# Half of the key transposes moved from TensorE to VectorE and DMA, and the convolution's taps shared by ScalarE and VectorE

## The chip, the cores and the metric

The kernel runs on one core of a Trainium2 chip. The metric is the time of one execution on the device in microseconds (us); lower is better. One profiled execution gives the rows below; its span runs from the first to the last instruction of the program.

## The reference

The input x has 8 sequences of 2048 tokens with 256 channels, in f32. Each token is normalised (xn), and the output is x + attention(xn) + ffn(xn).

- Attention: q, k, v = xn @ wqkv; q and k pass a relu; 16 heads of 16 channels. It is causal linear attention: for each token, num = q . cumsum(k v^T), den = q . cumsum(k) + 1e-5, y = num / den, and y @ wo.
- FFN: a router of 8 scores (sigmoid of xn @ Wr) picks the best two per token and scales them to a sum of one. Four of the eight experts are MLPs, silu(xn @ Wg) * (xn @ Wu) @ Wd with 128 hidden channels; two more give xn, one gives relu(xn), one gives nothing. To this a causal depthwise convolution of four taps over the tokens is added, with a bias: conv[n] = b + sum over i of w[i] * xn[n - 3 + i].

## The kernel before

The work goes in 32 batches of 512 tokens (T = 4 tiles of 128), four batches to a sequence; I number them 0 to 31. `rounds` (L229) calls one function `batch(s, j, left)` per engine for every batch; all loops are unrolled, and each engine has its own order of instructions, tied to the others by semaphores. `at` (L235) turns a batch and a count into the value of a semaphore. Inside a batch the argument k says for which batch a step works: k = 0 the present one, k = 1 the next, k = 2 or 3 those behind.

TensorE's batch (L433 to L556) has three stages:

1. For each tile t of four (tile and expert have the same number): `gate_up(t)`, twelve products of 512 columns in three passes of high and low halves into two ring banks; then `numerators(t)`, which holds many small products (L466, L482) and two `state_sum` steps (L429). `numerators(t)` waits for silu(t) of ScalarE. Behind tile 0 stand the second half of the masked scores (L415).
2. `heads(s, j, 1)` (L366) for the next batch: value and router products, then two key projections into score banks 0 and 1 and two query projections, and then the key transposes: eight of 128x128 (L397, T = 4 for each of two groups of channels), since `state_sum` needs keys with tokens on partitions (`ktok`).
3. `output(t)` for four tiles: the convolution is turned (L488), attention and the four experts are added up.

ScalarE (L632): silu, the high halves of hid (`high_hid`) and of y (`high_y`), the first tap with the bias (L654), the copies of the heads out of PSUM, relu terms. Its order is written out in L658 to L689. VectorE (L907): state_bd (L902), the gate product (L924), attend (L933), masks (L895), and taps 1 to 3 of the convolution, each two scalar_tensor_tensor of 128x512 (L916) that add to cT; then the statistics of a later batch, the router (L827), key sums, the products for the denominators, and the additions to x_t (L976). GpSimd: weighing hid by the router, low halves, normalising.

From batch 4 on (`by_blocks`, L248) xn isn't transposed on TensorE. VectorE turns it in blocks of 32x32 (`turn_x`, L850) into xb_t, a view of qks_tok, and SP puts the blocks in place with 32 DMAs of 16 KB per batch (`place_turned`, L302, L311). `products` (L866) waits until these have landed, since it writes qks_tok. SP then waits for the router and spreads its weights (`spread_cw`, L287: four small DMAs to DRAM, and one of 1 MB back), stores the finished batch (L321), waits for that, and loads the batch four ahead (L330).

In batches 3 to 30 TensorE's queue has 38 waits on a semaphore that was reached long ago (L538, FILL = 38), at the top of the batch. Two such waits become one instruction of the queue.

Statistics (VectorE) and `normalise` (GpSimd) for the batch two ahead stand at the end of batches 0 and 1; in batch 1 a second pair, for batch 4, stands behind them, after the last addition to x_t.

Of the kernel before, what the change touches and what calls it, by code (L numbers as in the profile page):

```python
# [16 lines left out]
def layer_kernel(nc, x, wqkv, wo, w_router, router_bias, w_gate, w_up, w_down, conv_w, conv_b,  # L17
# [13 lines left out]
    FILL = 38  # L31
# [18 lines left out]
    with ExitStack() as ctx:  # L50
# [85 lines left out]

        rdT = qks
# [26 lines left out]
        KTB = SB[0:2]  # L164

# [36 lines left out]
        s_ktok = sem("s_ktok")  # L202
        s_qp = sem("s_qp")
# [21 lines left out]
        s_conv = sem("s_conv")  # L225
        s_op = sem("s_op")
# [21 lines left out]
        def by_blocks(s, j, k):  # L248

            return s * BPS + j + k >= BY_PE  # L250

# [19 lines left out]
        def _(sp):  # L271
# [15 lines left out]
            def spread_cw(s, j, k):  # L287

                sp.wait_ge(s_cw, at(s, j, 1, k + 1))
                for b in range(P // BLK):  # L290
                    bs = slice(b * BLK, (b + 1) * BLK)
                    sp.dma_start(cw_rows[:, bs], cwt[b * BLK:b * BLK + E * T, :]).then_inc(cw_out, 16)
                sp.wait_ge(cw_out, at(s, j, 16 * P // BLK, (k + 1) * 16 * P // BLK))
# [8 lines left out]
            def place_turned(s, j, k):  # L302

                sp.wait_ge(s_turn, at(s, j, 1, k + 1 - BY_PE))

                sp.wait_ge(s_halo, at(s, j, 1, k - 1))
                for c in range(C):
                    for a in range(QUADS):
                        for q in range(QUADS):
                            row = xT[q * BLK:(q + 1) * BLK, third(s, j, k), c, LEAD:LEAD + BT]  # L310
                            sp.dma_start(row.rearrange("p (t a n) -> p t a n", t=T, a=QUADS)[:, :, a, :],  # L311
                                         xb_t[a * BLK:(a + 1) * BLK, c, q, :, :]).then_inc(xT_in[c], 16)

            def batch(s, j, left):
                b = s * BPS + j
                if left > 1 and by_blocks(s, j, 2):
                    place_turned(s, j, 2)
                if left:
                    spread_cw(s, j, 1)
                    sp.wait_ge(s_out, at(s, j, T, 2 * T))  # L320
# [15 lines left out]
        def _(pe):  # L336
# [29 lines left out]
            def heads(s, j, k):  # L366
# [19 lines left out]
                if not k:  # L386
                    pe.wait_ge(w_split, EARLY)
                for g in range(C):
# [5 lines left out]
                for g in range(C):  # L394
                    pe.wait_ge(s_kT, at(s, j, C, k * C + g + 1))
                    for t in range(T):
# [22 lines left out]
            def state_sum(s, j, k, n):  # L419
# [4 lines left out]
                t, h = n // 2, n % 2  # L424
                toks = slice(h * HALF, (h + 1) * HALF)
# [7 lines left out]
            def batch(s, j, left):  # L433
# [101 lines left out]
                if not last and by_blocks(s, j, 1):  # L535


                    for _ in range(FILL):  # L538
                        pe.wait_ge(tables_in, 16)
# [28 lines left out]
        def _(act):  # L568
# [28 lines left out]
            def heads(s, j, k):  # L597
# [13 lines left out]
                for g in range(C):  # L611
                    act.wait_ge(s_ktr, at(s, j, C, k * C + g + 1))
                    copy(ktok[:, :, g, :], KTB[g][:, :].rearrange("p (t n) -> p t n", t=T)).then_inc(s_ktok, 1)
# [18 lines left out]
            def batch(s, j, left):  # L632
# [24 lines left out]

                silu(0)  # L658
# [10 lines left out]
                high_y(0)  # L669
                silu(1)  # L670
                high_hid(0)
                high_y(1)
                if not last and not ahead:
                    lead(s, j, 1)
                silu(2)
                if not last and not ahead:
                    for c in range(C):
                        high_x(s, j, 1, c)
                high_hid(1)
                high_y(2)  # L680
                silu(3)
                high_hid(2)
                high_y(3)
# [31 lines left out]
        def _(pool):  # L715
# [34 lines left out]
            def batch(s, j, left):  # L750
# [39 lines left out]
                if left > 1 and not by_blocks(s, j, 2):  # L790
# [11 lines left out]
        def _(dve):  # L802
# [54 lines left out]

            def key_sums(s, j, k):
# [48 lines left out]
            def batch(s, j, left):  # L907
                last = left == 0

                def tap(n):  # L910
                    if n == 1:
# [26 lines left out]
                for t in range(T):  # L938
# [23 lines left out]
                if not last:  # L962
                    router(s, j, 1)
                    key_sums(s, j, 1)
# [104 lines left out]
```

## Time and profile before

| | us |
|---|---|
| median of 3 runs (1308.15 to 1309.69) | 1308.89 |
| the profiled execution | 1308.92 |
| its span | 1307.1 |
| PE busy (24160 matmuls) | 1287.2 (98%) |
| PE weight load | 1116.5 (85%) |
| DVE (VectorE) | 1144.3 (88%) |
| ACT (ScalarE) | 707.8 (54%) |
| POOL (GpSimd) | 830.8 (64%) |

Busy shares are of the span. A row of a timeline is: start in us from the span's start, duration in us, engine, line, operation, tiles written and read, shapes, count, and in brackets idle time of the engine before it with what ended it. Instructions of one kind that overlap are merged into one row, so "x4" with 2.48 us is four from the first start to the last end. DMAs have the engine's name with a q: the row is the time that the issue took in the queue, not the transfer.

### The profile page before, as it was taken

How to read it: one execution, taken by the hardware profiler on the slowest of the kernel's cores; microseconds unless marked ns; L12 is line 12 of the kernel's file. 1: busy time of each engine (PE TensorE's matmuls, PEld its weight loads, DVE VectorE, ACT ScalarE, POOL GpSimd, SP SyncE). 2: the span in 40 equal slices, each digit the busy share in tenths (PEclk: the TensorE clock that was granted, in tenths of full speed). 3: DMA queues.
4: the chain of work that ended last, by engine and by line, in shares of the span. 5: the costliest groups of instructions: out<-in, count | busy, mean ns of one | idle time of the engine just before them, and what ended most of it. 6: DMA issues, size and time to landing. Idle time of an engine off the chain costs nothing.

```text
span 1307.1 us, 55818 instructions
## 1 busy us (share of the span) xinstructions
PE 1287.2 (98%) x24160; PEld 1116.5 (85%) x24160; DVE 1144.3 (88%) x2686; ACT 707.8 (54%) x1487; POOL 830.8 (64%) x673
## 2 busy tenths in 40 slices
PE   5999999999999999999999999999999999999998
PEld 4888888888888888888888888888888888888887
DVE  7988898888898888988888988889888889888885
ACT  5645655455654456554555544565545555445552
POOL 2676665765666756657656667566576566675554
PEclk9999999999999999999999999999999999999999
DMA  5012212222222222222222222221222222222211
GB/s 185 14 56 73 78 50 51 80 78 78 65 61 56 79 78 79 51 51 81 78 79 64 67 51 78 78 78 51 51 80 78 79 64 67 51 78 63 61 35 34
DMA packets 175860, 88.54 MB, mean 68 GB/s; under 512 B 135552, under 2 KB 171264, under 8 KB 171520
## 3 DMA queue, kind: packets, MB, share of 16 engines
q1 hardware_dynamic: 174912, 83.97, 22.6%
q8 instruction: 191, 3.13, 1.0%
q10 hardware_dynamic: 704, 1.01, 0.2%
q14 instruction: 53, 0.43, 0.1%
HBM read 53.18 MB, written 17.04 MB: 54 GB/s over the span
## 4 chain that ended last, share of the span: by engine, by line
PE 95%; DVE 3%; POOL 1%; issue 1%; ACT 0%; DMA 0%; DVEq 0%; POOLq 0%
PE ring L343 51%; PE scores L343 17%; PE ring L466 7%; PE ring L482 6%; PE scores L415 5%; PE state_sum L429 4%; PE ring L488 2%; PE scores L397 2%; DVE sm L895 1%; POOL xn L731 0%; DMA x_t<-in_L_attn_x_dram 0%; PE scores L352 0%; POOL rstd L722 0%; DVE stats L819 0%; POOL x_t L748 0%
## 5 line engine op out<-in xcount | busy, mean ns | idle before, releaser
L757 POOL TENSOR_TENSOR hid<-hid,cwb 128x512 f32<-128x512 f32 x128 | 166.4, 1300 | 181.8 <-DVE hid L924 181.0
L916 DVE SCALAR_TENSOR_TENSOR cT<-xT,conv_ws,cT 128x512 f32<-128x512 f32 x192 | 275.1, 1471 | 0.0
L745 POOL TENSOR_TENSOR x_t<-x_t,same 128x1024 f32<-128x1024 f32 x32 | 76.9, 2404 | 254.9 <-ACT same L618 254.9
L639 ACT ACTIVATE sg<-ring 128x512 f32<-128x512 f32 x128 | 76.6, 599 | 268.5 <-PE ring L343 268.5
L343 PE MATMUL ring<-xl,wgu_h 128*128 128x512 f32 x512 | 213.1, 416 | 0.0
L761 POOL TENSOR_TENSOR hl<-hid,hh 128x512 fp32r<-128x512 f32 x128 | 208.8, 1632 | 0.0
L343 PE MATMUL ring<-xh,wgu_l 128*128 128x512 f32 x512 | 201.0, 393 | 0.3 <-issue 0.3
L343 PE MATMUL ring<-xh,wgu_h 128*128 128x512 f32 x512 | 200.5, 392 | 0.0
L569 ACT ACTIVATE yh<-yT 128x256 fp32r<-128x256 f32 x128 | 53.5, 418 | 246.7 <-DVE yT L933 246.7
L902 DVE TENSOR_TENSOR state_bd<-state_sum,tables_s 128x256 f32<-128x256 f32 x248 | 104.0, 419 | 93.8 <-PE state_sum L429 90.6
L895 DVE TENSOR_TENSOR sm<-scores,causal_s 128x512 f32<-128x512 f32 x256 | 157.7, 675 | 6.0 <-PE scores L415 5.0
L343 PE MATMUL ring<-wd_l,hh 128*128 128x256 f32 x496 | 139.3, 281 | 0.0
L343 PE MATMUL ring<-wd_h,hh 128*128 128x256 f32 x496 | 139.1, 280 | 0.0
L343 PE MATMUL ring<-wd_h,hl 128*128 128x256 f32 x496 | 139.0, 280 | 0.0
L766 POOL TENSOR_TENSOR yl<-yT,yh 128x256 fp32r<-128x256 f32 x128 | 135.3, 1057 | 0.0
L466 PE MATMUL ring<-sm,vp 64*32 64x64 f32 x8192 | 122.2, 225 | 0.0
L343 PEld LDWEIGHTS ring<-xl,wgu_h 128*128 128x128 f32 x512 | 96.1, 188 | 26.1 <-issue 5.5
L343 PEld LDWEIGHTS ring<-xh,wgu_l 128*128 128x128 f32 x512 | 96.4, 188 | 23.1 <-issue 0.8
L343 PEld LDWEIGHTS ring<-xh,wgu_h 128*128 128x128 f32 x512 | 96.6, 189 | 16.6
L466 PEld LDWEIGHTS ring<-sm,vp 64*32 64x32 f32 x8192 | 101.6, 105 | 2.8 <-issue 2.8
L343 PE MATMUL scores<-xh,wqk_h 128*128 128x512 f32 x256 | 100.2, 392 | 0.0
L343 PE MATMUL scores<-xl,wqk_h 128*128 128x512 f32 x256 | 100.2, 391 | 0.0
(134 smaller groups left out, 3453.4 us busy)
## 6 DMA issues: line engine op xcount, KB each, us to landing
cwb<-cw_rows SPq DMA_DIRECT2D x32, 1024.0 KB, 4.6
x_t<-in_L_attn_x_dram SPq DMA_DIRECT2D x32, 512.0 KB, 4.2
out_dram<-x_t SPq DMA_DIRECT2D x31, 512.0 KB, 2.9
xT<-qks_tok SPq DMA_DIRECT2D x896, 16.0 KB, 1.8
cw_rows<-cwt SPq DMA_DIRECT2D x128, 2.0 KB, 1.4
sm<-in_L_attn_wqkv_dram ACTq DMA_DIRECT2D x2, 384.0 KB, 5.0
sm<-in_L_ffn_Wg_dram SPq DMA_DIRECT2D x2, 256.0 KB, 3.8
sm<-in_L_ffn_Wu_dram SPq DMA_DIRECT2D x2, 256.0 KB, 4.6
```

Source lines behind the costliest of these rows:

```text
L343: ins = mm(dst, lhs, rhs, start=first and n == 0, stop=final and n == len(passes) - 1, skip_group_check=not (first and final))
L415: ins = mm(SB[f][h * HALF:(h + 1) * HALF, at_:at_ + P], kT[rows, g, n0:n0 + HALF], qp[rows, g, :, n0:n0 + HALF], start=True, stop=True)
L466: mm(NB2[t % 2][h][BLK * m:BLK * m + BLK, gs], window, sm[toks, t // 2, t % 2, 2 * pair + par, :], start=par == 0 and g == 0, stop=False, ...
L482: ins = mm(NB2[t % 2][h][rows, g * HALF:(g + 1) * HALF], state_bd[:, n % 4, cols], qT[:, g, n0:n0 + HALF], start=False, stop=True, skip_gr ...
L639: act.activation(sg[:, :], GB[t % 2], ACT.Silu).then_inc(s_sg, 1)
L745: pool.tensor_tensor(xb, xb, same[:, :, :], ALU.add).then_inc(s_base1, 1)
L757: pool.tensor_tensor(hid[:, e, :], hid[:, e, :], cwb[:, e, :], ALU.mult).then_inc(s_hid, 1)
L761: pool.tensor_tensor(hl[:, e, :], hid[:, e, :], hh[:, e, :].bitcast(F32), ALU.subtract).then_inc(s_hl, 1)
L766: pool.tensor_tensor(yl[:, :, t * P:(t + 1) * P], yT[:, t % 2, :, :], yh[:, :, t * P:(t + 1) * P].bitcast(F32), ALU.subtract).then_inc(s_y ...
L895: dve.tensor_tensor(heads, SB[f][:, :].rearrange("p (t a n) -> p t a n", a=2, n=HALF), causal2_s[:, :].unsqueeze(1).unsqueeze(1).to_broadc ...
L902: dve.tensor_tensor(state_bd[:, n % 4, :].rearrange("p (g m n) -> p g m n", g=C, m=PPG), ST.unsqueeze(2).to_broadcast([P, C, PPG, BLK]), s ...
L916: ins = dve.scalar_tensor_tensor(out=cT[:, c, :], in0=xT[:, third(s, j, 0), c, LEAD - HALO + n:LEAD - HALO + n + BT], scalar=conv_ws[:, c, ...
```

## The change

The diff, with unrelated context cut:

```diff
-    FILL = 38
+    FILL = 54
+        kb = hid[:, 2, :].rearrange("p (a t g i) -> p a t g i", a=QUADS, t=2, g=C)
+        TB = SB[0:2]
+        def keys_at(s, j, k):
+            return (s * BPS + j + k) * (16 * QUADS * QUADS)
...
 SP, spread_cw, between the four small DMAs and the wait for them:
+                if k:
+                    place_keys(s, j, k, range(1))
...
-            def place_turned(s, j, k):
+            def place_turned(s, j, k, c, quarters):
...
+            def place_keys(s, j, k, quarters):
+                sp.wait_ge(s_kturn, at(s, j, 1, k))
+                for a in quarters:
+                    for q in range(QUADS):
+                        sp.dma_start(ktok[a * BLK:(a + 1) * BLK, 2:4, :, q * BLK:(q + 1) * BLK],
+                                     kb[q * BLK:(q + 1) * BLK, a, :, :, :]).then_inc(ktok_in, 16)
 SP, batch:
-                    place_turned(s, j, 2)
+                    place_turned(s, j, 2, 0, range(QUADS))
+                    place_turned(s, j, 2, 1, range(QUADS // 2))
                 if left:
                     spread_cw(s, j, 1)
+                    place_keys(s, j, 1, range(1, QUADS))
...
 TensorE, heads:
+                if k and by_blocks(s, j, k):
+                    pe.wait_ge(s_conv, at(s, j, HALO, HALO))
                 for g in range(C):
                     project(KB[g][:, :], D + g * P).then_inc(s_kp, 1)
...
-                    for t in range(T):
+                    for t in range(T // 2 if k else T):
                         ins = nc.tensor.transpose(KTB[g][:, t * P:(t + 1) * P], kT[:, g, t * P:(t + 1) * P],
                                                   ident_s[:, :])
 TensorE, state_sum:
+                if n == T and s + j:
+                    pe.wait_ge(ktok_in, keys_at(s, j, k))
 TensorE, batch:
-                if not last and by_blocks(s, j, 1):
-                    for _ in range(FILL):
-                        pe.wait_ge(tables_in, 16)
+                def fill(n):
+                    if not last and by_blocks(s, j, 1):
+                        for _ in range(n):
+                            pe.wait_ge(tables_in, 16)
+                fill(FILL // 3)
...
                     if t == T - 1:
                         scores(s, j, 1, 0)
                         state_sum(s, j, 1, 0)
+                    elif t:
+                        fill(FILL // 3)
                     output(t)
...
 ScalarE, heads:
+                    some = T // 2 if k else T
+                    copy(ktok[:, 0:some, g, :], KTB[g][:, 0:some * P].rearrange("p (t n) -> p t n", t=some)
+                         ).then_inc(s_ktok, 1)
+            def place_turned(s, j, n):
+                if n == 0:
+                    act.wait_ge(s_turn, at(s, j, 1, 3 - BY_PE))
+                    act.wait_ge(s_halo, at(s, j, 1, 1))
+                a, q = QUADS // 2 + n // QUADS, n % QUADS
+                row = xT[q * BLK:(q + 1) * BLK, third(s, j, 2), 1, LEAD:LEAD + BT]
+                act.dma_start(row.rearrange("p (t a n) -> p t a n", t=T, a=QUADS)[:, :, a, :],
+                              xb_t[a * BLK:(a + 1) * BLK, 1, q, :, :]).then_inc(xT_in[1], 16)
 ScalarE, batch:
+                def tap_terms(n):
+                    if n == 1:
+                        act.wait_ge(s_sm, at(s, j, U * ROWS, U * ROWS))
+                    else:
+                        act.wait_ge(s_conv, at(s, j, HALO, n - 1))
+                    for c in range(C):
+                        first = LEAD - HALO + n
+                        ins = act.activation(TB[c][:, :], xT[:, third(s, j, 0), c, first:first + BT], ACT.Copy,
+                                             scale=conv_ws[:, c, n:n + 1])
+                    ins.then_inc(s_tapped, 1)
...
 GpSimd, batch, before weigh(1):
+                if by_blocks(s, j, 3) and not by_blocks(s, j, 2):
+                    normalise(s, j, 2)
...
-                if left > 1 and not by_blocks(s, j, 2):
+                if left > 1 and not by_blocks(s, j, 3):
                     normalise(s, j, 2)
 VectorE:
+            def turn_keys(s, j, k):
+                for g in range(C):
+                    dve.wait_ge(s_kT, at(s, j, C, k * C + g + 1))
+                dve.wait_ge(s_hl, at(s, j, T, 3))
+                for t in range(2):
+                    ins = dve.transpose(kb[:, :, t, :, :].rearrange("p a g i -> p g a i"),
+                                        kT[:, :, (2 + t) * P:(3 + t) * P].rearrange("p g (a n) -> p g a n", n=BLK))
+                ins.then_inc(s_kturn, 1)
+                def add_terms(n):
+                    if n == 1:
+                        dve.wait_ge(s_tap0, at(s, j, 1, 1))
+                    else:
+                        dve.wait_ge(s_conv, at(s, j, HALO, n - 1))
+                    dve.wait_ge(s_tapped, (s * BPS + j - BY_PE + 1) * HALO + n)
+                    for c in range(C):
+                        ins = dve.tensor_tensor(cT[:, c, :], TB[c][:, :], cT[:, c, :], ALU.add)
+                    ins.then_inc(s_conv, 1)
                 def tap(n):
+                    if not last and by_blocks(s, j, 1):
+                        add_terms(n)
+                        return
...
 gate_up(2) waits for the keys of the present batch, whose blocks lay in hid[:, 2]:
+                    if t == 2 and s + j:
+                        dve.wait_ge(ktok_in, keys_at(s, j, 0))
...
                         mask(s, j, 0, 1)
+                        if by_blocks(s, j, 3) and not by_blocks(s, j, 2):
+                            statistics(s, j, 2)
...
-                if left > 1 and not by_blocks(s, j, 2):
+                if left > 1 and not by_blocks(s, j, 3):
                     statistics(s, j, 2)
                 elif left > 2:
                     statistics(s, j, 3)
                 if not last:
                     router(s, j, 1)
+                    turn_keys(s, j, 1)
...
-                if by_blocks(s, j, 3) and not by_blocks(s, j, 2):
-                    statistics(s, j, 3)
```

The keys of tiles 2 and 3 of each next batch are turned by VectorE in blocks of 32x32 into the room of hid's third expert, and 16 DMAs from SP put the blocks in place. TensorE turns tiles 0 and 1 only. In batches 3 to 30 taps 1 to 3 are multiplied by ScalarE into score banks 0 and 1 and added by VectorE. Where SP placed 32 blocks of x, it now places 24, and ScalarE issues the other eight between its activations. ScalarE's order in a batch becomes: silu(1), place 0, high_hid(0), place 1, tap_terms(1), place 2, high_y(1), place 3, silu(2), place 4, high_hid(1), place 5, tap_terms(2), place 6, high_y(2), place 7, silu(3), high_hid(2), tap_terms(3), high_y(3). The filling waits stand at three places, 18 each: at the top of the batch, before output(1) and before output(2). Batch 3's statistics stand inside batch 1, behind the masks of its first tile, and its normalisation before weigh(1); batch 4's take the place that batch 3's had.

## Rows read from the trace of the kernel before

**Rows 1.** The page, part 4: the chain that ended last, share by engine.
```profile
PE 95%; DVE 3%; POOL 1%; issue 1%; ACT 0%; DMA 0%; DVEq 0%; POOLq 0%
```
**Rows 2.** The chain of waits in order of time: start us, us, what.
```profile
617.62 5.48 PE scores L343 x24
657.53 5.48 PE scores L343 x24
663.01 0.87 PE scores L397 x8
```
**Rows 3.** Busy time of each engine in one batch's stretch.
```profile
674.60:714.40 39.80, 39.80 (x755) 34.52 (x753) 35.81 (x85) 21.82 (x46) 26.05 (x22) 1.00 0.26 69
```
**Rows 4.** Timeline of VectorE, batch 16: start us, us, what.
```profile
679.56 1.41 DVE L854 STREAM_TRANSPOSE qks_tok<-xn 128x256 f32<-128x256 f32 x4
...
694.61 3.05 DVE L916 SCALAR_TENSOR_TENSOR cT<-xT,conv_ws,cT 128x512 f32<-128x512 f32 x2
...
699.57 0.18 DVE L830 TENSOR_TENSOR scoreb<-score,bias_s 128x32 f32<-128x32 f32 x1
...
702.63 0.12 DVE L848 TENSOR_TENSOR c<-cw 128x4 f32<-128x4 f32 x1
...
714.76 0.42 DVE L976 TENSOR_TENSOR x_t<-ring,x_t 128x256 f32<-128x256 f32 x1
```
**Rows 5.** Groups of instructions: busy us, mean ns of one, idle before.
```profile
L916 DVE SCALAR_TENSOR_TENSOR cT<-xT,conv_ws,cT 128x512 f32<-128x512 f32 x192 | 275.1, 1471 | 0.0
...
L924 DVE TENSOR_TENSOR hid<-ring,sg 128x512 f32<-128x512 f32 x128 | 87.0, 680 | 0.0
...
L654 ACT ACTIVATE cT<-xT,conv_bs,conv_ws 128x512 f32<-128x512 f32 x64 | 48.3, 804 | 0.0
```
**Rows 6.** Timeline of SP's queue in batch 16, and the page's store.
```profile
681.00 23.90 SPq L311 DMA_DIRECT2D xT<-qks_tok  x32
704.94 1.98 SPq L292 DMA_DIRECT2D cw_rows<-cwt  x4
...
715.21 0.40 SPq L321 DMA_DIRECT2D out_dram<-x_t  x1
...
out_dram<-x_t SPq DMA_DIRECT2D x31, 512.0 KB, 2.9
```
**Rows 7.** Timeline of ScalarE, batch 16.
```profile
686.65 0.60 ACT L639 ACTIVATE sg<-ring 128x512 f32<-128x512 f32 x1 [0.70 <-PE ring L343]
...
691.36 0.60 ACT L639 ACTIVATE sg<-ring 128x512 f32<-128x512 f32 x1 [0.70 <-PE ring L343]
691.86 0.62 ACT L569 ACTIVATE hh<-hid 128x512 fp32r<-128x512 f32 x1
```
**Rows 8.** Timeline of PE, batch 16: first and last gate products.
```profile
674.68 0.43 PE L343 MATMUL ring<-xl,wgu_h 128*128 128x512 f32 x1
...
692.29 0.39 PE L343 MATMUL ring<-xh,wgu_l 128*128 128x512 f32 x1
```
**Rows 9.** First DMA issues; ScalarE's semaphore instruction and the activation it passes.
```profile
0.71 0.43 ACTq L691 DMA_DIRECT2D tables_s<-in_tables_dram  x1
...
0.72 0.43 SPq L272 DMA_DIRECT2D x_t<-in_L_attn_x_dram  x1
...
L638 ACTq EVENT_SEMAPHORE  x96: 17/17/17, 37.8 to 1289.7; - x96
...
37.80 0.42 ACT L569 ACTIVATE yh<-yT 128x256 fp32r<-128x256 f32 x1 [2.23 <-DVE yT L933]
```
**Rows 10.** Source view of the filling waits: ns min/median/max, first and last start.
```profile
L539 PEldq EVENT_SEMAPHORE  x504: 51/51/51, 152.6 to 1233.7; - x168
```
**Rows 11.** Timeline of PE in batch 3, gate_up(1).
```profile
161.54 0.50 PE L343 MATMUL ring<-xh,wgu_l 128*128 128x512 f32 x1 [0.34 <-issue]
```
**Rows 12.** Timeline of batch 2: VectorE and PE.
```profile
119.35 1.43 DVE L854 STREAM_TRANSPOSE qks_tok<-xn 128x256 f32<-128x256 f32 x4 [1.60 <-POOL xn L731]
...
123.53 0.33 PE L429 MATMUL state_sum<-vp,ktok 64*32 64x32 f32 x16 [1.19 <-DVE state_bd L902]
```
**Rows 13.** Timeline of VectorE in batch 1.
```profile
80.90 0.42 DVE L902 TENSOR_TENSOR state_bd<-state_sum,tables_s 128x256 f32<-128x256 f32 x1 [0.79 <-PE state_sum L429]
```

More of the change, by code:

```diff
@@ L202, in layer_kernel @@
         s_ktok = sem("s_ktok")
+        s_kturn = sem("s_kturn")
+        ktok_in = sem("ktok_in")
         s_qp = sem("s_qp")
@@ L225, in layer_kernel @@
         s_conv = sem("s_conv")
+        s_tapped = sem("s_tapped")
         s_op = sem("s_op")
@@ L300, in spread_cw @@
                              cw_rows.rearrange("r n -> (r n)").partition_broadcast(P)).then_inc(cw_in, 16)
-            def place_turned(s, j, k):
+            def place_turned(s, j, k, c, quarters):
                 sp.wait_ge(s_turn, at(s, j, 1, k + 1 - BY_PE))
                 sp.wait_ge(s_halo, at(s, j, 1, k - 1))
[L307 to L312, printed above, removed]
+                for a in quarters:
+                    for q in range(QUADS):
+                        row = xT[q * BLK:(q + 1) * BLK, third(s, j, k), c, LEAD:LEAD + BT]
+                        sp.dma_start(row.rearrange("p (t a n) -> p t a n", t=T, a=QUADS)[:, :, a, :],
+                                     xb_t[a * BLK:(a + 1) * BLK, c, q, :, :]).then_inc(xT_in[c], 16)
+            def place_keys(s, j, k, quarters):
+                sp.wait_ge(s_kturn, at(s, j, 1, k))
+                for a in quarters:
+                    for q in range(QUADS):
+                        sp.dma_start(ktok[a * BLK:(a + 1) * BLK, 2:4, :, q * BLK:(q + 1) * BLK],
+                                     kb[q * BLK:(q + 1) * BLK, a, :, :, :]).then_inc(ktok_in, 16)
             def batch(s, j, left):
@@ L612, in heads @@
                     act.wait_ge(s_ktr, at(s, j, C, k * C + g + 1))
-                    copy(ktok[:, :, g, :], KTB[g][:, :].rearrange("p (t n) -> p t n", t=T)).then_inc(s_ktok, 1)
+                    some = T // 2 if k else T
[9 more added lines that the diff above has]
+                              xb_t[a * BLK:(a + 1) * BLK, 1, q, :, :]).then_inc(xT_in[1], 16)
             def same_terms(s, j, k):
@@ L669, in batch @@
                 high_y(0)
+                placing = left > 1 and by_blocks(s, j, 2)
                 silu(1)
+                if placing:
+                    place_turned(s, j, 0)
                 high_hid(0)
+                if placing:
+                    place_turned(s, j, 1)
+                if ahead:
+                    tap_terms(1)
+                if placing:
+                    place_turned(s, j, 2)
                 high_y(1)
+                if placing:
+                    place_turned(s, j, 3)
                 if not last and not ahead:
@@ L675, in batch @@
                 silu(2)
+                if placing:
+                    place_turned(s, j, 4)
                 if not last and not ahead:
@@ L679, in batch @@
                 high_hid(1)
+                if placing:
+                    place_turned(s, j, 5)
+                if ahead:
+                    tap_terms(2)
+                if placing:
+                    place_turned(s, j, 6)
                 high_y(2)
+                if placing:
+                    place_turned(s, j, 7)
                 silu(3)
                 high_hid(2)
+                if ahead:
+                    tap_terms(3)
                 high_y(3)
```

## The prediction

> **What bounds the kernel now.** I read the page's engine sums first, then the chain of waits, then the order of one steady batch on each engine. The chain that ends last is 95% PE, 3% DVE, 1% each POOL and issue [rows 1]. The marker is the block of 24 query and key products, 5.48 us: it starts at 617.62 and again at 657.53, so a batch lasts 39.91 us, and behind each block stand the eight key transposes, 0.87 us [rows 2]. The stretch that shows it best has TensorE busy for all of its 39.80 us, at the full granted clock; VectorE works 35.8 us of it, ScalarE 21.8, GpSimd 26.1 [rows 3]. So only two things change the time: matmuls taken off TensorE, and a wait that becomes so late that TensorE runs dry.
>
> **Part 1: the keys of tiles 2 and 3 leave TensorE.** In each of the 31 batches that prepare a next one (k = 1) four of eight 128x128 transposes go. One costs 0.87 / 8 = 0.109 us [rows 2], so a batch loses 0.435 us and the kernel 31 x 0.435 = 13.5 us, as long as nothing becomes late. What comes instead:
> - VectorE: two block transposes of 128x256 behind the router. The same shape elsewhere takes 1.41 us for four [rows 4], so 0.7 us; I take 0.8 (bounds 0.7 and 1.4, the latter if the scattered order in which both groups are read makes them twice as dear).
> - SP: 16 DMAs more, but eight of the 32 for x go to ScalarE, so 40 instead of 32 in SP's batch. 32 took 23.90 us, 0.75 each on average [rows 6]. The 24 for x would last from 681.0 to 698.9, inside the wait for the router (c at 702.63 [rows 4]). Four small ones of cw take 1.98 us, four keys 3.0: cwb goes at about 707.8. Twelve keys take 9.0 us, until 717. The store of the finished batch moves from 715.21 to 717, its landing 2.9 us later lets the load go at about 720.5 instead of 718.3, and the next x blocks are turned at 721. SP has no waiting left, but nothing is late: the last keys land before 720 (the store, far larger, needs 2.9), and the first TensorE instruction that waits for them, the state sum of tile 2, comes some 9.3 us into the next batch, near 723.5. 4 us of cover; I cost it at nothing. If the cover goes, each microsecond of lateness is one of the batch: 31 us a microsecond.
> - ScalarE copies half of the keys: 2 x 0.2 us saved where it doesn't count.
>
> **Part 2: taps split.** A tap now is 3.05 us of VectorE at its longest, three a batch [rows 4]. It becomes a product on ScalarE into two score banks and an addition on VectorE. The addition reads PSUM and SBUF like the gate product, 0.68 us (L924 [rows 5]) against 1.47 (L916 [rows 5]): with two halves a tap 3 x 2 x 0.79 = 4.7 us come back to VectorE in 28 batches, for which it pays 0.8. It isn't the bound; that gives TensorE nothing by itself. It only pays for the key transposes: the router may start when the last score is out (ACT table and sigmoid end near 698.9) instead of at 699.57, so its end moves from 702.75 to 702.1, the turned keys end at 702.9 and everything behind stands where it stood, while TensorE is 0.44 us earlier. The last addition to x_t ended at 715.2 [rows 4]; TensorE needs it at the numerators of the next batch, 2.9 us behind its first gate product, which is at 674.68 [rows 8] + 39.8 = 714.5: 717.4, now 717.0. Cover 1.7 us.
> ScalarE: no row shows it writing such a product to PSUM; 128x512 takes it 0.62 (the copy of hid [rows 7]) to 0.80 us (the first tap [rows 5]). I take 1.4 for a pair, nearer to the first tap, which also scales by a column. The new waits: TensorE waits for all taps before the key products, which start with the block at 697.3 (657.53 + 39.8). The last addition starts where the last tap did, 694.61 [rows 4], and ends at 695.9. Cover 1.3 us, queued behind it is all of TensorE. The product before it waits for the second tap (691.5) and the third activation of hid (691.86 to 692.4 [rows 7]), so it ends at 693.9, before high_y(3) at 694.72.
>
> **Part 3: eight DMA issues on ScalarE,** four between silu(1) and silu(2), four up to silu(3). This is the edit I trust least, since TensorE's numerators wait for silu. Its last gate product of tile 3 starts at 692.29 [rows 8], the numerators 0.3 behind it, and silu is ready at 691.96 [rows 7]: 0.6 us of cover. Lower bound: the issue runs in the queue while the engine works. For this speaks that ScalarE's own semaphore instruction of L638 passes at 37.8, just when the activation starts that stands in front of it and runs until 38.2 [rows 9]. Then silu is not late, cost 0. Upper bound: the engine stands still. From silu(2) to silu(3), 4.71 us apart [rows 7], lie activations of 0.5 (silu, to the copy of hid that follows), 0.5, 1.4 and 0.4 us and 4 x 0.75 of issue: 5.8 us, or 5.4 with 0.65 an issue. After two intervals silu(3) is 1.4 to 2.1 us late, less the cover 0.7 to 1.5 us, in 28 batches 20 to 40 us. I take 0, as the row of L638 is the nearest.
> A rule of the Trainium skill speaks against it (Perfetto Trace Analysis, section on the HWDGE DMA instruction): the descriptor generator is shared and locked for one issuer, and the profiled time includes the wait for the lock. The rows show the opposite where both issue at once: 0.43 us on ScalarE at 0.71 and 0.43 on SP at 0.72, no longer than the ones alone [rows 9]. By the rows the sum stays; by the rule it is the second rival below.
>
> **Part 4: filling waits.** 38 at one place become 18 at each of three. A pair is one queue instruction of 51 ns (504 of them stand under L539 [rows 10]); 19 of them cost TensorE nothing, as the gate product behind them, at 674.68, has no idle time before it [rows 8]. Nine behind 18 such products are covered the better. Cost 0; if the cover were gone 27 x 0.1 = 2.7 us a batch at most, which no row supports. What they may do is shift instruction blocks: with the four transposes eight instructions go, with the waits eight come. Once, in batch 3, TensorE stood 0.5 us in gate_up(1) with no releaser but issue [rows 11]; that may vanish or stay. I take -0.25.
>
> **Part 5: statistics of the fourth batch sooner.** Batch 2 lost 1.3 us: xn of batch 4 came too late from GpSimd, VectorE waited 1.60 us for it at 119.35, and TensorE 1.19 us for state_bd at 123.53 [rows 12]. Now batch 3's statistics (1.9 us, as from the end of the tap, 697.66, to the router, 699.57 [rows 4]) stand in batch 1 behind the masks, which ended 0.79 us before 80.90, where state_bd of chunk 4 then started [rows 13]; it starts at 82.05 instead and ends at 82.5. TensorE took it within 0.1 us of its end before, so up to 1.1 us is lost there. GpSimd normalises before weigh(1), 3 us of work, but hl is due 10 us after. Net -0.2 (bounds -1.3 and +0.5). The extra 0.8 us of key turning in batches 0 to 2, without cheaper taps, has 2 us of cover.
>
> **Sum.** 1307.1 - 13.5 - 0.25 - 0.2 = 1293.1 us span. The profiled execution took 1308.92, 1.8 more, and the median of the runs is 1308.89: the same. That is 1294.9; forecast 1295 us, 1.1% less.
>
> **Rivals.**
> A. ScalarE stands while it issues. For: the interleaving leaves no room to catch up between silu(1) and silu(3), four issues in each 4.7 us. Against: the L638 row. It decides from about 0.3 us an issue. Time: 1295 + 20 to 40, some 1322, slower.
> B. The issue engine is shared, and SP issues without pause from 681. An issue on ScalarE then lasts 1.3 us in the queue, four 5.2 us where 4.7 is there: 0.5 to 1 us a batch late after two intervals, the cover of 0.6 off: 0.2 to 0.5 us, x28 is 6 to 14 us. Time 1301 to 1309. Against: the simultaneous issue at 0.71.
> C. The keys or SP take the gain: behind the 1 MB spread of cwb (4.6 us to land on the page) the small key blocks queue, and each batch waits at its third tile. It needs over 4 us of lateness; then 1295 + 31 x 0.4 = 1308, no change.
> D. More is won than I count: both early losses and the small spread between batches (39.8 to 40.1) vanish. 1292.
>
> **Chances.** Forecast with D 0.73, B 0.08, A 0.12, C 0.07. A measurement of this kernel tells about 0.2%, 2.6 us, from no change. Faster 0.82 (the forecast, D, B's lower half and some of C that still gains), same 0.06, slower 0.12. The range: the unknown early terms give 1292 to 1296; partial stalls on ScalarE and B's lower half reach to 1302. 1290.5 to 1302.
>
> **What would show it.** Blocks of 24 products 39.5 us apart instead of 39.9; L397 with 132 instead of 256 matmuls; no wait of TensorE for conv or the keys; silu still right behind its gate product in the ScalarE order, and hh right behind silu. Wrong if PE has idle time released by sg (A, B), by the DMA of ktok (C), or if batches 1 and 2 together still lose more than 1.3 us.

## The result, and the profile after

The changed kernel takes 1312.15 us (median of 13 runs, 1310.71 to 1313.8) against 1308.95 (13 runs). The ratio is 1.0025, 95% interval 1.0018 to 1.0032: slower by 0.25%, where 1295 was forecast, and outside the range. The profiled execution has a span of 1312.0 us.

The page first, engine sums and chain. Compared with [rows 1], TensorE's share of the chain is unchanged. DVE and GpSimd have less work than before (80% and 58% of the span for 88% and 64%), ScalarE has more (62% for 54%), and none of them is a bound. So nothing stands out: the loss lies within "TensorE is busy".

```profile
PE 1290.1 (98%) x24036; PEld 1116.3 (85%) x24036; DVE 1051.0 (80%) x2748; ACT 807.2 (62%) x1655; POOL 756.5 (58%) x673
...
PE 95%; DVE 2%; POOL 1%; issue 1%; ACT 1%; DMA 0%; DVEq 0%; POOLq 0%
```

Busy time by stretch (span, then busy us and count of PE, PEld, DVE, ACT, POOL, granted clock, DMA share, GB/s). The first is a steady batch, to be held against [rows 3]; the second is batch 1, which took 40.83 us before.

```profile
680.02:719.75 39.73, 39.73 (x750) 34.36 (x749) 32.06 (x86) 25.46 (x52) 23.29 (x22) 1.00 0.31 76
71.62:118.38 46.76, 42.41 (x766) 36.48 (x765) 38.81 (x95) 22.28 (x48) 31.25 (x29) 0.96 0.19 55
```

I then took from the PE timeline the start of each batch's first gate product, and of each run of like products within it. Before, batches 4 to 29 average 39.95 us; after, 40.03, although each has four transposes less. Batch 30 alone shows what was forecast: 39.51, from 40.01. Batch 1 is 5.93 longer, batch 2 is 1.35 and batch 3 0.53 shorter.

Inside a batch every stretch has its old length but three. The transposes went from 0.87 to 0.43 us. The small products behind the gate of tile 1, and again of tile 2 (state sums and numerators, 96 products with a weight load each; call them S1 and S2), took 1.14 us in every steady batch before; after, they average 1.39 and 1.43. Here is S2 of batch 16 before (core timeline of PE: start us, us, what): from 687.92 to 689.05.

```profile
687.92 0.25 PE L429 MATMUL state_sum<-vp,ktok 64*32 64x32 f32 x5
...
688.07 0.84 PE L466 MATMUL ring<-sm,vp 64*32 64x64 f32 x59
688.80 0.33 PE L429 MATMUL state_sum<-vp,ktok 64*32 64x32 f32 x16
689.05 0.34 PE L482 MATMUL ring<-qT,state_bd 128*64 128x64 f32 x4
```

The same after, S1 of batch 16 (688.49 to 689.72, 1.23, one of the mildest) and the middle of its S2 (56 products now take 1.08, where 59 took 0.84). No row has an idle time: the stream is only thinner.

```profile
688.49 0.25 PE L459 MATMUL state_sum<-vp,ktok 64*32 64x32 f32 x5
...
688.63 0.98 PE L496 MATMUL ring<-sm,vp 64*32 64x64 f32 x59
689.41 0.33 PE L459 MATMUL state_sum<-vp,ktok 64*32 64x32 f32 x16
689.72 0.70 PE L512 MATMUL ring<-qT,state_bd 128*64 128x64 f32 x16
...
693.45 1.08 PE L496 MATMUL ring<-sm,vp 64*32 64x64 f32 x56
```

What stands beside it, ScalarE and the two queues. The issues overlap the activations, and silu comes right behind its gate product (ACT L686, released by PE): the lower bound of Part 3 was right about ScalarE. But one issue of ScalarE lies inside each of S1 and S2, where SP issues as well. SP issued through S1 and S2 before, too [rows 6], with no effect.

```profile
686.33 18.61 SPq L324 DMA_DIRECT2D xT<-qks_tok  x24
...
687.23 0.60 ACT L686 ACTIVATE sg<-ring 128x512 f32<-128x512 f32 x1 [1.81 <-PE ring L366]
687.29 0.59 ACTq L659 DMA_DIRECT2D xT<-qks_tok  x1
687.93 0.63 ACT L604 ACTIVATE hh<-hid 128x512 fp32r<-128x512 f32 x1
...
688.70 0.69 ACT L714 ACTIVATE scores<-xT,conv_ws 128x512 f32<-128x512 f32 x1
688.71 0.61 ACTq L659 DMA_DIRECT2D xT<-qks_tok  x1
```

Batch 1 is an ordinary chain of waits. GpSimd normalises ahead of its second weighing (four tiles in 3.11 us; the next normalisation takes 2.16), ScalarE waits 3.08 and 3.16 us for hid, its copies of the scores are late, TensorE stands in the query products, DVE's router is late, and at 114.48 TensorE waits 1.85 us for DVE. One link was in nobody's sum: the pair of DVE products at 107.94 took 3.50 us, beside an addition of GpSimd that began 0.18 us behind its start; without the early normalisation (e14 below) the same pair took 1.29, and the addition began 1.06 us behind its start. These 2.2 us are more than the last wait. That the addition is the cause is inferred from the two times only.

```profile
83.19 3.11 POOL L814 TENSOR_SCALAR xn<-x_t,negm,rstd 128x256 f32<-128x256 f32 x4
...
94.15 0.63 ACT L604 ACTIVATE hh<-hid 128x512 fp32r<-128x512 f32 x1 [3.08 <-POOL hid L840]
98.25 0.63 ACT L604 ACTIVATE hh<-hid 128x512 fp32r<-128x512 f32 x1 [3.16 <-POOL hid L840]
...
100.69 0.50 PE L366 MATMUL scores<-xl,wqk_h 128*128 128x512 f32 x1 [1.48 <-ACT score L636]
...
107.94 3.50 DVE L965 TENSOR_TENSOR qks<-qT,ksum 128x512 f32<-128x512 f32 x2
...
108.12 2.77 POOL L828 TENSOR_TENSOR x_t<-x_t,same 128x1024 f32<-128x1024 f32 x1 [6.74 <-ACT same L665]
...
114.48 0.44 PE L518 MATMUL ring<-tables_s,cT 128*128 128x128 f32 x2 [1.85 <-DVE x_t L1092]
```

The last wait costs more than itself. In the stretches around it (the column after the five engines is the granted clock) TensorE works 0.63 us of the 2 us from 112 and 1.52 of the next two; from 116 to 118 the clock is 0.50, the 1.2 GHz level, and the last 18 products take 3.73 us instead of 2.22.

```profile
112.00:114.00 2.00, 0.63 (x43) 0.35 (x29) 1.97 (x4) 0.00 (x0) 2.00 (x2) 1.00 0.98 317
114.00:116.00 2.00, 1.52 (x9) 1.52 (x10) 1.97 (x6) 1.54 (x2) 1.90 (x4) 0.71 0.22 32
116.00:118.00 2.00, 2.00 (x11) 2.00 (x11) 2.00 (x5) 0.00 (x0) 0.90 (x2) 0.50 0.16 25
118.00:120.00 2.00, 2.00 (x11) 1.73 (x10) 1.92 (x5) 0.01 (x1) 0.00 (x0) 0.93 0.05 8
```

Sum of what changed: 31 x 0.435 = 13.5 won; about 26 x 0.54 = 14.0 lost in S1 and S2 of batches 4 to 29 and 0.9 more in batches 2 and 3; 5.93 + 0.43 lost in batch 1 (it won its transposes too); 1.9 won in the pauses of batches 2 and 3. That makes +5.9; the spans differ by 4.9 (1307.1 to 1312.0), the rest lies in hundredths of a microsecond per batch, such as the gate products of tile 0 (2.86 for 2.88).

### The profile page after: what moved, and what is told of

Read it like the earlier page. It is cut to its first block, busy times and chain, and to the rows that moved or that the text cites. A ratio compares the mean times of both kernels' runs of the same rounds, so it can differ in the third digit from the quotient of the medians.

```text
span 1312.0 us, 56722 instructions
## 1 busy us (share of the span) xinstructions
PE 1290.1 (98%) x24036; PEld 1116.3 (85%) x24036; DVE 1051.0 (80%) x2748; ACT 807.2 (62%) x1655; POOL 756.5 (58%) x673
## 3 DMA queue, kind: packets, MB, share of 16 engines
q8 instruction: 191, 3.13, 1.0%
## 4 chain that ended last, share of the span: by engine, by line
PE 95%; DVE 2%; POOL 1%; issue 1%; ACT 1%; DMA 0%; DVEq 0%; POOLq 0%
PE ring L366 51%; PE scores L366 17%; PE ring L496 7%; PE ring L512 6%; PE scores L442 5%; PE state_sum L459 5%; PE ring L518 2%; PE scores L424 1%; POOL hid L840 0%; DMA x_t<-in_L_attn_x_dram 0%; DVE qks L965 0%; POOL xl L821 0%; POOL xn L814 0%; POOL hl L844 0%; POOL yl L849 0%
## 5 line engine op out<-in xcount | busy, mean ns | idle before, releaser
L686 ACT ACTIVATE sg<-ring 128x512 f32<-128x512 f32 x128 | 76.6, 599 | 256.8 <-PE ring L366 256.7
L844 POOL TENSOR_TENSOR hl<-hid,hh 128x512 fp32r<-128x512 f32 x128 | 170.4, 1331 | 0.0
L496 PE MATMUL ring<-sm,vp 64*32 64x64 f32 x8192 | 129.5, 225 | 0.0
L714 ACT ACTIVATE scores<-xT,conv_ws 128x512 f32<-128x512 f32 x168 | 109.1, 683 | 6.7 <-issue 1.8
L496 PEld LDWEIGHTS ring<-sm,vp 64*32 64x32 f32 x8192 | 106.9, 105 | 4.7 <-issue 2.8
L459 PEld LDWEIGHTS state_sum<-vp,ktok 64*32 64x32 f32 x3968 | 64.0, 106 | 53.7 <-issue 47.8
L1013 DVE TENSOR_TENSOR cT<-scores,cT 128x512 f32<-128x512 f32 x168 | 107.3, 680 | 0.0
```

The lines of the kernel that those rows point to most:

```text
L459: ins = mm(ST[rows, g, :], ktok[toks, t, g, rows], vp[toks, t, g * PPG + m, 0:3:2, :], start=first and g == 0, stop=True, skip_group_check ...
L496: mm(NB2[t % 2][h][BLK * m:BLK * m + BLK, gs], window, sm[toks, t // 2, t % 2, 2 * pair + par, :], start=par == 0 and g == 0, stop=False, ...
L686: act.activation(sg[:, :], GB[t % 2], ACT.Silu).then_inc(s_sg, 1)
L714: ins = act.activation(TB[c][:, :], xT[:, third(s, j, 0), c, first:first + BT], ACT.Copy, scale=conv_ws[:, c, n:n + 1])
L844: pool.tensor_tensor(hl[:, e, :], hid[:, e, :], hh[:, e, :].bitcast(F32), ALU.subtract).then_inc(s_hl, 1)
L1013: ins = dve.tensor_tensor(cT[:, c, :], TB[c][:, :], cT[:, c, :], ALU.add)
```

## The experiments

Theory 1: ScalarE's issues beside SP's thin the stream of small products. Rivals: the filling waits or the place of the instruction blocks (2), ScalarE's tap products (3). "Batches 4 to 29" below is their mean period in us, and so is a number near 40 that stands alone behind a ratio. The kernel before, timed beside these runs, has medians of 1308.6 to 1309.0.

**e1, issues elsewhere.** The eight `place_turned` calls stand behind `tap_terms(1)` (2), `high_y(1)`, `tap_terms(2)` (2), `high_y(2)` and `tap_terms(3)` (2).

> The changed kernel, but ACT's 8 DMA issues per batch stand where the tensor engine is in gate_up products of 12 and not in the small products behind the gates of tiles 1 and 2 (each such stretch, numerators and state sums, took 1.14 us before and 1.38 to 1.59 in the changed kernel). Theory 1 (an issue on ACT's queue beside SP's slows the stream of small matmuls): both stretches return to 1.14, the period of batches 4 to 29 falls from 40.0 to 39.5, the kernel takes 1298 to 1299. Theory 2 (the filling waits, or where the instruction stream falls, slow the stretches) and theory 3 (ACT's products with the taps, written into PSUM, do it): stretches stay at 1.4 to 1.6, 1311 to 1313.

1308.19 us, ratio 0.9995 (0.9985 to 1.0005); batches 4 to 29: 39.83. S1 fell to 1.17, S2 only to 1.29, and the stretch of tile 3 rose from 0.91 to 1.06. Several moved issues slid into the neighbouring stretches. It speaks for theory 1, but settles nothing.

**e2, keys by ScalarE.**

```diff
-                    place_turned(s, j, 2, 1, range(QUADS // 2))      # SP
+                    place_turned(s, j, 2, 1, range(QUADS))
...
-                    place_keys(s, j, 1, range(1, QUADS))
+                    place_keys(s, j, 1, range(1, 2))
...
                     denominators(s, j, 1)                            # ScalarE
+                    place_keys(s, j, 1, range(2, QUADS))
```

> The changed kernel, but SP issues all 32 blocks of x, and ACT issues 8 of the 16 blocks of keys instead, behind the denominators' copy, in its idle 5 us of the output stage. Theory 1: no issue on ACT in the stretches behind the gates, so 1.14 again, 1298 to 1299; small products of the output stage (scores and a state sum, 0.9 us) may pay up to 0.3 per batch for it, 1307 at most. Theories 2 and 3: 1311 to 1313. If SP becomes the bound with 6 us more of x issues (cw later by 3.3 us, POOL's first weighing late), a wait of the tensor engine for DVE or POOL appears in each batch and the time is over 1305 with stretches of 1.14.

1305.46, ratio 0.9973 (0.9963 to 0.9983), 39.60. S1 and S2 are back at 1.15 and 1.14 with taps, fills and keys as in the changed kernel: rivals 2 and 3 are out for this loss. SP issues in S1 and S2 as before, ScalarE no longer does. The time stayed above 1299 for other reasons: batch 1 took 48.3, and the table load stood behind eight issues in a row (5.76 us), so silu(0) was late:

```profile
710.47 5.76 ACTq L656 DMA_DIRECT2D ktok<-hid  x8
716.26 1.28 ACT L683 ACT_TABLE_LOAD   x1 [5.54 <-issue]
```

**e3, statistics back.** Part 5 undone, everything else as changed.

> The changed kernel with the part on the fourth batch's statistics and normalisation undone (they stand where they stood before). Theory A (POOL's early normalisation of 3.1 us and DVE's statistics in batch 1 make batch 1 5.9 us longer): batch 1 returns to 40.9 to 41.3, the stall of batch 2 (1.4 us) and the pause of batch 3 (0.5) come back, total 1308 to 1309. Theory B (the fills, or the steady loss, lengthen batch 1 too): batch 1 stays over 44, total 1311 to 1314.

1308.88, ratio 1.0001 (0.9992 to 1.0011): batch 1 40.4, batch 2 42.6, batch 3 39.9. Theory A.

**e4, the kernel before with 8 of 32 x blocks issued by ScalarE.**

```diff
                 silu(1)
+                place_turned(s, j, 0)
                 high_hid(0)
+                place_turned(s, j, 1)
+                place_turned(s, j, 2)
...
```

(and five more, up to `high_y(2)`)

> The kernel before, with nothing changed but that 8 of the 32 blocks of x in each batch are issued by ACT, at the places that the changed kernel has. Theory 1: the small products behind the gates of tiles 1 and 2 go from 1.14 to 1.4 to 1.6 us in the batches in which x is placed, +0.7 us in 29 of 32 batches against none saved elsewhere: 1320 to 1326. Theories 2 and 3: no change, 1308 to 1310.

1319.98, ratio 1.0085 (1.0068 to 1.0102), 40.31 against 39.95. This one edit alone costs 11 us. S1 and S2 average 1.31 and 1.35, and they come in two kinds. In batch 5 both queues are held in drawn-out issues through the whole stretch, and it takes 245.50 to 246.64, 1.14; in batch 8 both issue freely, and it takes 365.39 to 366.73, 1.34:

```profile
244.57 2.94 SPq L310 DMA_DIRECT2D xT<-qks_tok  x3
244.96 2.54 ACTq L622 DMA_DIRECT2D xT<-qks_tok  x2
...
245.50 0.24 PE L429 MATMUL state_sum<-vp,ktok 64*32 64x32 f32 x5
...
246.64 0.34 PE L482 MATMUL ring<-qT,state_bd 128*64 128x64 f32 x4
...
364.50 3.26 SPq L310 DMA_DIRECT2D xT<-qks_tok  x4
364.83 1.25 ACTq L622 DMA_DIRECT2D xT<-qks_tok  x2
365.39 0.24 PE L429 MATMUL state_sum<-vp,ktok 64*32 64x32 f32 x5
...
366.73 0.45 PE L482 MATMUL ring<-qT,state_bd 128*64 128x64 f32 x8
```

**e5, both losses taken out:** e2 with the statistics back, and ScalarE's eight key issues spread: two behind `same_terms`, two behind `relu_terms`, four behind `denominators`.

> Keys by ACT (as e2, but its 8 issues spread: 2 behind same, 2 behind relu, 4 behind the denominators) and the statistics of the fourth batch back where they stood (as e3). If the two losses are separate: period of batches 4 to 29 is 39.5 (e2 39.60, of which 0.1 is the late silu behind 8 issues in a row), batch 1 40.4, batch 2 near 42, sum 1308.8 - 26 x 0.45 - 1 = 1296 to 1298. If SP with its 32 blocks is the real limit in e2 (0.1 per batch): 1299 to 1301. If something else than the two holds the rest: over 1302.

1295.05 (1294.92 to 1295.39), ratio 0.9895 (0.9879 to 0.9912), 39.51. The forecast's time, and nearly its terms: the 13.5 us of the transposes and the pause of batch 3 are in it, Part 5 isn't.

**e6, the early preparation in another place:** statistics behind tap 1, GpSimd's normalisation behind `weigh(3)`, the next statistics behind `products`.

> As e5, with the third batch's data prepared early again, but the statistics behind the first tap and POOL's normalisation behind its fourth weighing, and the next batch's statistics behind the products. If the stall of batch 2 (1.4 to 2 us) can be had without the 5.9 us of batch 1: batch 1 within 0.5 of 40.4, batch 2 40.5 instead of 42, 1.0 to 2 us below e5. If POOL's 3.1 us hurt anywhere ahead of the heads: batch 1 at 42 or more, and the time at or above e5.

1301.94, ratio 0.995 (0.9933 to 0.9966). A miss: batch 1 took 49.3. Batch 2 was 40.35, so its stall can be removed, but not at this price: TensorE waited 3.7 us for DVE's additions to x_t and 2.7 for state_bd.

**e7 and e8, ScalarE issues added to the kernel before,** eight a batch at the places of e4, into a tile nobody reads.

```diff
+                act.dma_start(aside[n:n + 1, 0:32], tables_s[0:1, 0:32])                # e7
+                act.dma_start(aside[:, n * 16:(n + 1) * 16], tables_s[:, 0:16])         # e8
```

> The kernel before, plus 8 DMA issues per batch on ACT's queue at the places of the changed kernel, each of one packet of 128 bytes into a tile that nobody reads. Theory 1a (it is the transfer's burst of 128 packets that holds up the stream of small matmuls): S(1) and S(2) stay at 1.14 and the span at 1307 to 1309. Theory 1b (the issue itself, on a second queue, does it): S(1) and S(2) at 1.3 to 1.6, the span at 1316 to 1320.

> As e7, but each of the 8 added transfers has 128 packets of 64 bytes (8 KB, half the bytes of a block of x, as many packets). Theory 1a with packets as the cause: S(1) and S(2) at 1.3 to 1.6, the span at 1314 to 1320. Theory 1a with bytes as the cause: half of the slowing, 1.2 to 1.3. Theory 1b: the same as e7, slow in both.

1318.75 and 1318.65 (one run each), 40.30 and 40.29; S1 and S2 1.28 and 1.34, 1.29 and 1.33. A transfer of ScalarE of 128 bytes costs as much as one of 8 KB or, in e4, 16 KB: it isn't the size of what ScalarE moves. Groups by line for e7 (busy us, mean ns), to hold against 122.2 and 81.6 us in the kernel before:

```profile
L468 PE MATMUL ring<-sm,vp 64*32 64x64 f32 x8192 | 126.6, 225 | 0.0
L431 PE MATMUL state_sum<-vp,ktok 64*32 64x32 f32 x3968 | 90.2, 198 | 1.7 <-DVE state_bd L926 1.6
```

**e10, the same tiny issues in batches 1 and 30 only,** where SP issues nothing in S1 and S2.

> The kernel before, plus the 8 tiny issues of e7, but only in batches 1 and 30, in which SP issues no blocks of x and so none in the small products of tiles 1 and 2. If it takes two queues issuing at once: these stretches stay at 1.14 in both batches. If an issue on ACT's queue does it alone: 1.25 to 1.4 as in e7.

1308.60 (one run). S1 and S2 are 1.14 in both batches, with ScalarE issuing inside them for 0.54 to 0.70 us. So ScalarE's issues don't do it alone, as SP's don't (before, e2, e5); it takes both queues. In these two batches SP's transfers of x are missing along with its issues, and no run parts the two. S1 of batch 30:

```profile
1246.95 0.61 ACTq L621 DMA_DIRECT2D aside<-tables_s  x1
1247.03 0.24 PE L431 MATMUL state_sum<-vp,ktok 64*32 64x32 f32 x5
...
1247.90 0.33 PE L431 MATMUL state_sum<-vp,ktok 64*32 64x32 f32 x16
1248.16 0.45 PE L484 MATMUL ring<-qT,state_bd 128*64 128x64 f32 x8
```

**e9, e5 with the mask ahead of the turning of x in batch 2.**

```diff
-                            turn_x(s, j, 2)
+                            if not late: turn_x(s, j, 2)      # late: batch 2 only
                         mask(s, j, 0, 1)
+                        if late: turn_x(s, j, 2)
```

> As e5, but in the third batch (batch 2) DVE takes the mask of its second scores first and turns x behind it, so that POOL's normalisation, for which the turning waits 1.6 us, is done by then. If that wait is what makes batch 2 42.3 instead of 40.4 us: 1.2 to 1.8 less than e5, 1293.3 to 1294. If the turned x or SP's blocks are then late for batch 3: batch 3 over 39.8 and the time as e5, 1295.

1293.86 (1293.14 to 1294.19), ratio 0.9886 (0.9869 to 0.9902): the best version found. DVE's turning has no wait any more where it had 1.60 us [rows 12], and batch 2 fell from 42.3 to 41.4 us. DVE's timeline in batch 2:

```profile
118.74 2.48 DVE L971 TENSOR_TENSOR sm<-scores,causal_s 128x512 f32<-128x512 f32 x4 [0.70 <-PE scores L442]
121.14 1.41 DVE L920 STREAM_TRANSPOSE qks_tok<-xn 128x256 f32<-128x256 f32 x4
```

**e11, e5 with the taps whole on DVE; e15, the same on e9.**

> As e5, with the taps whole on DVE again, as before (no products on ACT, no wait for them ahead of the keys' products). If DVE has room for the turning of keys (0.8 us) without it, as the row of its idle time says: 1295 to 1296. If the split is what gives the turned keys their room: the output stage waits for DVE, 0.1 to 1 us per batch, 1298 to 1320. Theory 3 (ACT's products slow the small matmuls): below e5.

> e9 (1293.9) with the taps whole on DVE as in e11 (1294.5 where e5 had 1295.1). If both small gains are real and apart: 1293.0 to 1293.6. If the split of the taps is worth nothing either way: 1293.9 as e9.

1294.49, ratio 0.989 (0.9874 to 0.9907), and 1294.13, ratio 0.9887 (0.9871 to 0.9904). Without the split of the taps e5 gets 0.6 us faster and e9 0.3 us slower, both under 0.1%: it is worth nothing either way.

**e12, e5 with 38 filling waits at the top and none else; e13, with all 54 at the top.**

> As e5, with the filling waits as they were before, 38 ahead of the gate products and none in the output stage. If they only fill time in which the tensor engine would wait: no difference, 1295. If their places matter for the instruction stream: the rates of the small products or the gaps between tiles change, by up to 0.1 us per batch, 1292 to 1298.

> As e5, with all 54 filling waits ahead of the gate products (e12: 38 there, which took 1316.2, with a pause of 1.0 to 1.7 us in the first scores of batches 13 to 27, ended by nothing but issue). Theory N (the number of instructions per batch matters: with 8 fewer than e5 the start of each block of 256 wanders through the batch and comes into the scores): no pause, 1295 to 1296. Theory P (the place matters, the waits of the output stage give the front of the instruction stream its rest): the pause is there as in e12, 1310 to 1320.

e12: 1316.20, ratio 1.0056 (1.004 to 1.0073), 21 us above e5 and far outside what was expected. From batch 13 to 27 the first scores take 1.9 to 3.0 us instead of 1.14, with a hole that wanders by a few products from batch to batch:

```profile
677.32 0.67 PE L442 MATMUL scores<-qp,kT 32*64 32x128 f32 x27
679.12 0.89 PE L442 MATMUL scores<-qp,kT 32*64 32x128 f32 x37 [1.14 <-issue]
```

e13: 1320.65, ratio 1.0093 (1.0076 to 1.011). That hole is gone, as theory N has it, but the time isn't N's: another is there in batches 3 to 30, in front of the first gate product, where all 54 waits stand: it starts 0.92 to 1.00 us behind the last product of the batch before instead of 0.12. This one is the time of the waits themselves. The trace has their 27 instructions 0.106 us apart, 2.9 us in all, and the last 18 products, beside which they run, last 2.2; the 19 of e12 need 2.0 and fit. (The profile puts TensorE's wait down to x_t, the weight load's to issue.)

```profile
680.82 0.47 PE L366 MATMUL ring<-xl,wgu_h 128*128 128x512 f32 x1 [0.71 <-DVE x_t L1068]
...
680.78 0.19 PEld L366 LDWEIGHTS ring<-xl,wgu_h 128*128 128x128 f32 x1 [0.88 <-issue]
```

Waits of the weight loads (us in total, times, longest) in e13, then in e12:

```profile
PEld ring L366 <- issue: 29.3, 60, 0.9
```
```profile
PEld ring L366 <- issue: 6.2, 32, 0.8
```

**e14, only the statistics early,** GpSimd's normalisation where it stood.

> The changed kernel, but only DVE's statistics of the fourth batch stand early; POOL's normalisation and the next batch's statistics stand where they stood before. If DVE's 2 us are the loss of batch 1: 42 or more. If POOL's early 4.1 us (reciprocal root and normalisation ahead of its second weighing) are the greater part: 41.5 or less, of which 1.1 is the state block that is 1 us late.

1308.64 (one run); batch 1 41.5, batch 2 42.2. DVE's statistics cost 1.1 us in batch 1 (e3 has 40.4); the other 5.2 us of the 46.8 come with GpSimd's normalisation. The edit moves batch 4's statistics on DVE as well, from ahead of the router to behind the additions; in the changed kernel DVE waited 2.21 us for the scores behind them, so they held nothing up.

**e16, the kernel before with 54 filling waits at the top.**

> The kernel before with 54 filling waits instead of 38, which is 8 instructions more per batch (1541.75 instead of 1533.75, six blocks of 256 are 1536). Theory N: the block starts wander 5.75 earlier per batch instead of 2.25 later, and reach a dense stretch in some batches: pauses of 1.0 to 1.7 us there, 1312 to 1325. Theory P, and the view that the waits only fill idle time: 1308 to 1310.

1374.67, ratio 1.0487 (1.0459 to 1.0515). That is 66 us, four times the largest loss expected: the hole behind the 54 waits of e13, and holes of up to 2.6 us in the first scores, moving by some nine products from one batch to the next; the mean granted clock fell from 0.999 to 0.988 besides:

```profile
PEld scores L415 <- issue: 32.8, 22, 2.6
PEld ring L343 <- issue: 32.7, 62, 1.3
PE scores L415 <- issue: 25.2, 21, 2.3
```

Where the holes in the scores stand can be counted. I number TensorE's instructions in the order of the program, weight loads, products and waits. Of every idle time of the weight loads over 0.45 us, from batch 3 to the last product, the first instruction behind it has number 193 or 194 in its block of 256 in all 15 of e12, in 22 of 27 of e16 (the other five, 0.65 us or less, follow one of these within some 6 us), and in the single one of the kernel before [rows 11]. The changed kernel, e5 and e13 have none. Each of these holes ends 1.2 to 1.6 us after an instruction packet of 16 KB has landed. So these holes are TensorE waiting for its instructions, and theory N was right about them. A steady batch of e12 has 1526.75 instructions, one of e5 1534.75: by the distance to 1536, six blocks, the same place in a block moves 9.25 instructions a batch in e12 and 1.25 in e5, and in e12 it comes into the scores.

## Why the prediction was wrong, point by point

**What bounds the kernel: right.** In a steady batch TensorE has no idle time before, after, or in e5. What was missed is that a busy TensorE can be slower, in stretches of many small products (96 in 1.14 us), while the 24 large ones keep their 5.48 us.

**Part 1, 13.5 us for the transposes: right.** 39.95 to 39.51 in e5 is 0.44 a batch where 0.435 was worked out, and no wait for the keys appeared (rival C is out).

**Part 3, "I take 0" for the eight issues on ScalarE: the step that failed first.** Both bounds were drawn around ScalarE, whether silu would be late. It wasn't (rival A, out). The price, 0.25 to 0.3 us in each of S1 and S2, falls on TensorE, and only where the two queues issue at once (e2, e4, e7, e8, e10): 14 to 15 us, more than Part 1 wins. Rival B gave 1301 to 1309 by another mechanism, a late silu, which the rows don't show: an issue of ScalarE lasts 0.59 to 0.61 us while SP issues. By the rule on the HWDGE lock (the Trainium skill, Perfetto Trace Analysis, section on the HWDGE DMA instruction) two issuers would lengthen each other; in most rows here they don't. The drawn-out issues of e4 don't decide it, as SP alone needed 0.75 on average before [rows 6].

**Part 5, net -0.2 with bounds of -1.3 and +0.5: failed.** Batches 1 to 3 together are 4.6 us longer than in e3, which lacks only this part (3.3 in the medians). The 1.1 us of the late state block was right (e14). Of the prediction's own signs of being wrong, two stayed away (idle time released by sg, or by the DMA of ktok) and the third came: batches 1 and 2 lost far more than 1.3 us. "3 us of work, but hl is due 10 us after" was the error: what is due next isn't hl but hid, which ScalarE takes in order ahead of the copies of the next batch's scores. 3.1 us of GpSimd became 5.2 of the batch, 1.5 of them through the clock, behind a wait that the 2.2 us of the slower DVE products can account for. The gain in batch 2 came as written (1.35 for 1.3).

**Part 4, cost 0: right for the change, partly by luck.** The remark that eight instructions go and eight come was the point, and I priced it at nothing. Without the eight (e12) 21 us are lost; with them at one place (e13) 26. The upper bound "if the cover were gone" was real for 54 waits in a row: a wait takes 0.106 us of the queue, not its 51 ns, and 27 of them outlast the products beside them. The pause of batch 3 went, 0.5 us where I took 0.25.

**Part 2, no gain: right** (e11, e15). It isn't needed for the turned keys either.

**What stays open.** Why two queues slow the stream, and one doesn't, wasn't found. The runs exclude the size of ScalarE's transfer and either queue by itself; they don't part SP's issues from SP's transfers. The instruction packets aren't it either: in e7, S1 and S2 average 1.31 with such a packet on its way and 1.31 without. In the holes of e12 and e16 it isn't known why the supply fails in and beside the scores and hardly ever where instruction 193 of a block falls among the large products; that large products leave it more time is a guess, untested.

## What to carry to other kernels

When work is moved to another queue to relieve one engine, look at what the bounding engine does in those microseconds: long products don't notice, a stream of small ones does, so put the issues beside the long ones or in an idle tail (e5). When instructions leave a loop that is bound by TensorE, compare where the gaps marked issue fall before and after; replacing them by waits may be worth more than the edit. Before moving work ahead on an engine that has idle time, follow what it delays in the order of every engine that waits for it, not only its own last product.

## What the hardware showed that was not expected

- Small products (64x64 and 64x32, 1.14 us for 96, so 12 ns from one to the next) slowed to 1.2 to 1.6 us for 96 with issues on ScalarE's and SP's queues together; the 24 large query and key products stayed at 5.48 us in the steady batches of every version.
- The page counts 191 instruction packets in 3.13 MB, beside 49,080 instructions of TensorE before: about one per 256.
```profile
q8 instruction: 191, 3.13, 1.0%
```
- A steady batch has 1533.75 instructions before and 1534.75 after on average, next to six times 256; with 1526.75 (e12) the kernel is 21 us slower than e5, with 1541.75 (e16) 5% slower than before. The holes stand at the 193rd instruction of a block, 1.2 to 1.6 us behind the landing of a packet.
- 38 filling waits in a row, or 18 at each of three places, leave no gap; 54 in a row leave TensorE idle for 0.7 us. Two waits are one instruction of 51 ns, but the next starts 0.106 us after it.
- Behind one wait of 1.85 us the granted clock went to 0.50, and 18 products took 3.73 us instead of 2.22.
